# GpSimd's order within a step of the dense products, and 21 instead of 20 window additions per mixing tile

## The chip, the cores and the metric

The kernel runs on one core of one Trainium2 chip. The metric is device time in microseconds (us), the median of several executions. Engines are called PE (TensorE), PEld (its weight load), DVE (VectorE), ACT (ScalarE), POOL (GpSimd) and SP (SyncE, which here only starts transfers).

## The reference

A graph network layer by layer, on 1250 nodes with 1024 features and 40000 edges:

```python
h = jnp.maximum(_layernorm(x, axis=-1), 0.0)
x = x + h @ W.T + bias            # W: 1024 x 1024, W[src, dst] += edge_weight
h = jnp.maximum(_layernorm(x, axis=-1), 0.0)
# two layers on h, with deg the number of edges into a node:
agg = jax.ops.segment_sum(h[src], dst, num_segments=N)
h1 = relu(h @ W_self0 + (agg / max(deg, 1)) @ W_neigh0 + b0)
out = h1 @ W_self1 + (agg(h1) / max(deg, 1)) @ W_neigh1 + b1
x = x + out
```

All in float32. The kernel keeps the precision by splitting each operand into a rounded "hi" part and the rest, "lo", and summing three products of the parts.

## The kernel before

**Stages.** (1) 40 groups of 1000 edges are turned by matmuls into windows: small blocks of the edge-count matrix AT and of the sparse W. The windows of AT go to DRAM (`asum_scratch`) and come back later through a ring of four buffers, `az`. (2) W is turned, and the mixing runs over ten node tiles: x + h @ W.T. (3) Two layers, each with 35 steps of a seven-product scheme for h @ W, and then twenty products with the edge-count matrix (`neighbours`, L1425).

**The seven-product scheme.** Each layer has 7 panels of 5 steps; step v is panel p = (v mod 35) // 5 and row block i = v mod 5. A step is `product(v)`, 24 matmuls of 128x512 on PE (L1383). Its left operand is a transposed block of h, in `stage[v % 2]`, loaded by SP. In the panels p = 2, 3, 5, 6 that operand is first made by POOL from two blocks (`add_operands`, L862, L866, L868 and L871). Then ACT rounds it to hi (`operand_hi`, L1068) and POOL takes operand less hi to get lo (`operand_lo`, L880), into `split[v % 2]`. So the operand of step v + 1 is prepared while PE runs step v; ACT may begin on it only when product(v - 1) has ended, since `split` has two buffers.

**The right operands.** Each panel needs eight blocks of weights, 128x512. They are made one panel ahead, two in each of the steps i = 0 to 3 and none at i = 4 (`blocks_at`). For the panels 2 to 5, so in the steps of the panels 1 to 4, POOL makes a block by a subtraction (`add_blocks`, L895 and L897) from T and `wst`; ACT rounds it (`block_hi`, L1059), DVE takes the rest (`block_lo`, L1734). SP loads the blocks through the ring `wst` of four, each load when the lo of the block four before it is done, and in its queue the operand of step v + 2 stands behind the blocks of step v + 1.

**The window additions.** POOL adds the 288 windows to AT one by one (`add_asums`, L842). Every 16 additions it reads 16 places from the table `tab_a`. The additions are dealt out to 17 slots by `FIRST_ADD`: 40 in slot 0, `MIX_ADDS` each in the slots 1 to 10, the rest of the first 264 over three slots, and 8 each in the last three. In POOL's program the slots 0 to 10 stand in a row ahead of `operand_lo(0)`; slot 11 + v stands in step v. A slot's units (buffers of 4 to 12 windows) are loaded by SP: those of slot i + 1 ahead of right block i + 3 in its queue.

**Who waits.** The engines are separate queues in program order, tied by semaphores. PE's product(v) waits for hi and lo of its operand, at i = 0 also for the eight blocks of its panel, and for the emptied PSUM banks.

Of the kernel before, what the change touches and what calls it, by code (L numbers as in the profile page):

```python
# [19 lines left out]
TN = -(-N // NT)  # L20
# [38 lines left out]
SETS = [(0, 8), (8, 11), (11, 13), (13, 15), (15, 17)] + [(j, j + 1) for j in range(17, LATE)]  # L59
SET_OF = {j: w for w, (a, b) in enumerate(SETS) for j in range(a, b)}  # L60
TURN_ADDS = 40
MIX_ADDS = 20
LATE_AT = 2
FIRST_DEG = 7
AT_TOP = 20
# [10 lines left out]
VL = STEPS * PAIRS  # L76
# [26 lines left out]
NTH = {start: w for w, start in enumerate(STARTS)}  # L103
IN_MIXING = TURN_ADDS + MIX_ADDS * TN
FIRST_ADD = [0] + [TURN_ADDS + MIX_ADDS * i for i in range(TN)]
FIRST_ADD += [IN_MIXING + (len(EARLY_STARTS) - IN_MIXING) * v // (LATE_AT + 1) for v in range(LATE_AT + 2)]
# [3 lines left out]
def build_program(nc, x, x_cols, dst, src_cols, dst_cols, weight_cols, L0_gnn_bias, L1_gnn_W_self0, L1_gnn_W_neigh0,  # L110
# [10 lines left out]
    with ctx:  # L121
# [258 lines left out]
        def used(i, ring):  # L380

            return 16 * (i // ring + 1)


        def parts(v):

            layer, r = divmod(v, VL)
            return layer, r // PAIRS, r % PAIRS

        def op_loaded(v):  # L390

            return 16 * sum(len(LEFT[parts(u)[1]]) for u in range(v % 2, v + 1, 2))

        def nth_sum(v):

            layer, p, i = parts(v)
            return len(LEFT_SUMS) * PAIRS * layer + PAIRS * LEFT_SUMS.index(p) + i

        def source(v):

            layer, p, i = parts(v)
            return S[:, i, :] if p in (2, 3) else stage[:, v % 2, 0, :]
# [18 lines left out]
        def blocks_at(v):  # L421

            layer, p, i = parts(v)
            if p == STEPS - 1:
                return range(0)
            first = WB * (STEPS * layer + p + 1)
            return range(first + BLOCKS_AT[i][0], first + BLOCKS_AT[i][1])
# [40 lines left out]
        def g_at(layer, r):  # L468

            n = r - (VL - TN)  # L470
            return range(2 * TN * layer + n, 2 * TN * layer + n + 1) if 0 <= n < TN else range(0)

        def g_between(layer, o):
            first = 2 * TN * layer + TN
            return range(first + o - 1, first + (TN if o == TN - 1 else o)) if 1 <= o < TN else range(0)
# [11 lines left out]
        def load(eng, row, lo, hi):  # L487

            _, vals = nc.values_load_multi_w_load_instructions(
                row, engines=bass.OrderedEngineSet([eng.engine]), min_val=lo, max_val=hi,  # L490
                skip_runtime_bounds_check_because=clamped)
            return vals
# [16 lines left out]
        def ka(j):  # L509
            return WDS[j] * TN  # L510
# [76 lines left out]
        def adds_in(slot):  # L587
            return STARTS[FIRST_ADD[slot]:FIRST_ADD[slot + 1]] if slot + 1 < len(FIRST_ADD) else []
# [9 lines left out]
        def mix_done(eng):  # L598

            for i in range(TN - 2, TN):  # L600
                eng.wait_ge(s_x1d[i % 2], used(i, 2))
                eng.wait_ge(s_hd[i % 2], used(i, 2))
# [172 lines left out]
        def _(pool):  # L775
# [53 lines left out]
            def add_asums(slot):  # L829

                for j, c in adds_in(slot):
                    n, pos = UNIT_OF[(j, c)]
                    w, entry = NTH[(j, c)], GC * j + c
                    if entry % LOADS == 0:
                        a_bases[:] = load(pool, tab_a[0:1, entry:entry + LOADS], 0, N * TN // 2)
                    if pos == 0 and n < NS_A:
                        pool.wait_ge(s_az[n % NZ], used(n, NZ))
                    elif pos == 0:
                        pool.wait_ge(s_late, n - NS_A + 1)
                    pairs = ka(j) // 2  # L840
                    a = AT32[:, bass.ds(a_bases[entry % LOADS], pairs)]
                    pool.tensor_tensor(a, a, az32[:, n % NZ, pairs * pos:pairs * (pos + 1)], ALU.add) \  # L842
                        ._wait_ge(s_at, w).then_inc(s_at, 1)
# [7 lines left out]
            def add_operands(v):  # L851

                layer, p, i = parts(v)
                if p not in LEFT_SUMS:
                    return
                pool.wait_ge(s_hl[v % 2], op_loaded(v))
                if p == 2:
                    if layer == 0 and i == 0:
                        mix_done(pool)
                    elif i == 0:  # L860
                        pool.wait_ge(s_ag, OL)
                    last = pool.tensor_tensor(S[:, i, :], stage[:, v % 2, 0, :], stage[:, v % 2, 1, :], ALU.add)  # L862
                elif p == 3:
                    pool.wait_ge(s_ohi, v - PAIRS + 1)
                    pool.wait_ge(s_olo, v - PAIRS + 1)
                    last = pool.tensor_tensor(S[:, i, :], S[:, i, :], stage[:, v % 2, 0, :], ALU.subtract)  # L866
                elif p == 5:
                    last = pool.tensor_tensor(stage[:, v % 2, 0, :], stage[:, v % 2, 0, :], stage[:, v % 2, 1, :],  # L868
                                              ALU.subtract)
                else:  # L870
                    last = pool.tensor_tensor(stage[:, v % 2, 0, :], stage[:, v % 2, 0, :], S[:, i, :], ALU.subtract)  # L871
                last.then_inc(s_comb, 1)

            def operand_lo(v):
                if parts(v)[1] in LEFT_SUMS:
                    pool.wait_ge(s_comb, nth_sum(v) + 1)
                else:
                    pool.wait_ge(s_hl[v % 2], op_loaded(v))
                pool.wait_ge(s_ohi, v + 1)
                pool.tensor_tensor(split[:, v % 2, 1, :], source(v), split[:, v % 2, 0, :].bitcast(F32),  # L880
                                   ALU.subtract).then_inc(s_olo, 1)
# [26 lines left out]
            operand_lo(0)  # L908
            for layer in range(2):
                for v in range(VL * layer, VL * (layer + 1)):  # L910
                    ahead = v + 1 < VL * (layer + 1) and v != VL
                    if ahead:
                        add_operands(v + 1)
                    for c in blocks_at(v):
                        add_blocks(c)
                    if ahead:
                        operand_lo(v + 1)
                    add_asums(1 + TN + v)
                    for k in g_at(layer, v % VL - 1):
                        g_lo(k)  # L920
                for k in g_at(layer, VL - 1):
                    g_lo(k)
                for o in range(OL):
                    if layer == 1 and o >= 1:
                        store_out(pool, OL + o - 1)
                    for k in g_between(layer, o):
                        g_lo(k)
                    if layer == 0 and o == OL - 1:
                        operand_lo(VL)
                        operand_lo(VL + 1)  # L930
# [999 lines left out]
```

## Time and profile before

| | |
|---|---|
| median of 3 runs | 816.04 us (814.84 to 818.44) |
| time of the profiled execution | 816.04 us |
| its span | 813.9 us |
| PE busy | 786.5 us, 97% |
| DVE, ACT, POOL busy | 493.6, 366.9, 407.1 us |
| granted TensorE clock, mean | 0.996 of full |

The span is from the first to the last instruction on the core; 2.1 us of the time lie around it. PE is busy in nearly all of the span from 15 us on, so what matters are the few gaps in PE's row and the margin with which the other engines deliver the next step's operand.

### The profile page before, as it was taken

What the parts mean: (1) busy time and instruction counts of PE and PEld (TensorE: products, weight loads), DVE (VectorE), ACT (ScalarE), POOL (GpSimd) and SP (SyncE); (2) the same over time, 40 slices, a digit from 0 to 9 for tenths busy, and PEclk for the clock granted to TensorE, in tenths of its full rate; (3) what the DMA queues carried; (4) which work ended last, traced back from release to release, by engine and by line L of the source; (5) the groups of instructions that cost most, each with busy time, mean ns of one, the idle gap of its engine ahead of it and who ended that gap; (6) DMA issues with size and microseconds to landing.
All of it is one profiled execution on the core that took longest, in us unless ns stands there. A gap on an engine that the chain in (4) does not pass through costs nothing.

```text
span 813.9 us, 13261 instructions
## 1 busy us (share of the span) xinstructions
PE 786.5 (97%) x4533; PEld 638.4 (78%) x4534; DVE 493.6 (61%) x797; ACT 366.9 (45%) x482; POOL 407.1 (50%) x558
## 2 busy tenths in 40 slices
PE   2999999999999999999999999999999999999998
PEld 2766788888778788888877878888888888878886
DVE  7999577778443788876423443235559766246443
ACT  7665643334244232223237876543223223267653
POOL 3000055466758898764752210117899756724310
PEclk9999999999999999999999999999999999999999
DMA  3122455775555853577855643556844669668654
GB/s 109 41 69 80 134 171 168 235 249 165 171 203 187 299 181 90 181 233 244 290 191 175 213 156 106 188 172 213 291 143 142 203 186 340 229 199 267 222 163 140
DMA packets 83127, 151.40 MB, mean 186 GB/s; under 512 B 10965, under 2 KB 21068, under 8 KB 83056
## 3 DMA queue, kind: packets, MB, share of 16 engines
q1 hardware_dynamic: 61354, 102.49, 39.8%
q10 hardware_dynamic: 20182, 43.07, 15.0%
q0 software_dynamic: 1520, 4.92, 1.5%
q8 instruction: 40, 0.66, 0.3%
q14 instruction: 31, 0.25, 0.1%
HBM read 103.79 MB, written 46.65 MB: 185 GB/s over the span
## 4 chain that ended last, share of the span: by engine, by line
PE 86%; DVE 5%; issue 3%; DMA 2%; POOL 2%; ACT 1%; POOLq 0%; ACTq 0%; SPq 0%; DVEq 0%
PE bank L1383 44%; PE bank L1425 20%; PE bank L1318 12%; PE bank L1229 3%; PE bank L1218 3%; PE bank L1234 1%; PE bank L1213 1%; POOL AT L842 1%; PE bank L1441 1%; DVE L L1608 1%; PE bank L1311 1%; DVE R L1594 1%; PE bank L1266 1%; DMA b<-in_L_gnn_b 0%; POOL T L897 0%
## 5 line engine op out<-in xcount | busy, mean ns | idle before, releaser
L1383 PE MATMUL bank<-slot,split 128*128 128x512 f32 x1680 | 387.7, 392 | 3.8 <-issue 2.4
L1383 PEld LDWEIGHTS bank<-slot,split 128*128 128x128 f32 x1680 | 314.9, 189 | 70.1 <-issue 5.2
L842 POOL TENSOR_TENSOR AT<-AT,az 128x50 int32 (+3 forms) x288 | 95.5, 332 | 136.6 <-DMA az<-asum_scratch 97.7
L880 POOL TENSOR_TENSOR split<-stage,split 128x512 fp32r<-128x512 f32 x50 | 65.9, 1319 | 113.0 <-ACT split L1068 112.8
L1100 ACT CAST Ax<-AT 128x1280 fp32r<-128x1280 uint16 x40 | 106.9, 2673 | 32.1 <-PE bank L1425 20.4
L1734 DVE TENSOR_TENSOR slot<-T,slot 128x512 fp32r<-128x512 f32 x64 | 87.5, 1396 | 23.1 <-ACT slot L1059 21.9
L1318 PE MATMUL bank<-slot,split_m 128*128 128x512 f32 x320 | 91.2, 396 | 0.0
L1068 ACT CAST split<-stage 128x512 fp32r<-128x512 f32 x50 | 31.1, 624 | 123.6 <-PE bank L1383 61.1
L1734 DVE TENSOR_TENSOR slot<-wst,slot 128x512 fp32r<-128x512 f32 x48 | 46.6, 997 | 52.9 <-ACT slot L1059 52.9
L1425 PE MATMUL bank<-slot,Ax 128*128 128x512 f32 x320 | 77.2, 393 | 0.2
L1854 DVE SCALAR_TENSOR_TENSOR cst<-bank,dinv,stage 128x512 f32<-128x512 f32 x40 | 30.1, 752 | 72.8 <-PE bank L1425 72.3
L897 POOL TENSOR_TENSOR T<-T,wst 128x512 f32<-128x512 f32 x48 | 70.8, 1491 | 4.1 <-DMA wst<-in_L_gnn_W_self 4.1
L1425 PEld LDWEIGHTS bank<-slot,Ax 128*128 128x128 f32 x320 | 59.3, 188 | 12.9 <-issue 0.8
L1318 PEld LDWEIGHTS bank<-slot,split_m 128*128 128x128 f32 x320 | 58.5, 188 | 11.1
L1213 PE MATMUL bank<-L,R 125*128 125x40 bf16 (+3 forms) x296 | 41.4, 196 | 8.5 <-DVE L L1608 7.0
L1318 PE MATMUL bank<-WTlo,split_m 128*128 128x512 f32 x160 | 49.5, 391 | 0.0
L1425 PE MATMUL bank<-g_first,Ax 128*128 128x512 f32 x200 | 48.6, 389 | 0.0
L1059 ACT CAST slot<-T 128x512 fp32r<-128x512 f32 x64 | 38.1, 619 | 18.1 <-POOL T L897 12.2
L905 POOL TENSOR_TENSOR slot<-cst,slot 128x512 fp32r<-128x512 f32 x16 | 21.6, 1351 | 47.9 <-ACT slot L1115 47.9
L1068 ACT CAST split<-S 128x512 fp32r<-128x512 f32 x20 | 12.4, 622 | 71.8 <-PE bank L1383 63.0
L1213 PEld LDWEIGHTS bank<-L,R 125*128 125x128 bf16 x296 | 29.3, 99 | 19.2 <-issue 13.1
L1425 PEld LDWEIGHTS bank<-g_first,Ax 128*128 128x128 f32 x200 | 37.5, 188 | 7.9
(190 smaller groups left out, 1075.0 us busy)
## 6 DMA issues: line engine op xcount, KB each, us to landing
stage<-hT_scratch SPq DMA_DIRECT2D x90, 256.0 KB, 3.6
wst<-in_L_gnn_W_neigh SPq DMA_DIRECT2D x56, 256.0 KB, 4.7
wst<-in_L_gnn_W_self SPq DMA_DIRECT2D x56, 256.0 KB, 3.1
x1b_scratch<-x ACTq DMA_DIRECT2D x10, 512.0 KB, 5.4
hT_scratch<-hTs ACTq DMA_DIRECT2D x10, 512.0 KB, 3.0
stage<-prod0s_scratch SPq DMA_DIRECT2D x20, 256.0 KB, 2.8
hT_scratch<-h1s ACTq DMA_DIRECT2D x20, 256.0 KB, 3.2
stage<-prod1s_scratch SPq DMA_DIRECT2D x20, 256.0 KB, 2.8
```

The costliest lines, as they stand in the source:

```text
L842: pool.tensor_tensor(a, a, az32[:, n % NZ, pairs * pos:pairs * (pos + 1)], ALU.add) \
L880: pool.tensor_tensor(split[:, v % 2, 1, :], source(v), split[:, v % 2, 0, :].bitcast(F32), ALU.subtract).then_inc(s_olo, 1)
L897: last = pool.tensor_tensor(T[:, b, :], T[:, b, :], wst[:, c % NS, :], ALU.subtract)
L1059: act.copy(slot[t % 2][:, 0, HF * b:HF * (b + 1)], block_source(c)).then_inc(s_whi, 1)
L1068: act.copy(split[:, v % 2, 0, :], source(v)).then_inc(s_ohi, 1)
L1100: act.copy(Ax[:, o % 2, :, :], ATd[:, NT * n:NT * (n + 1), :].rearrange("p d s -> p s d")).then_inc(s_ax, 1)
L1213: last = pe.matmul(a_bank(n)[:, at:at + ka(j)], row, L[:, q, c, 0:ka(j)], start=(c % SHARED[j] == 0), stop=ends)
L1318: last = pe.matmul(bank[2 * (i % 2) + half][0:NT, :], split_m[:, i % 2, a, NT * k:NT * (k + 1)], WT[b][:, k, HF * half:HF * (half + 1)], s ...
L1383: last = pe.matmul(dense_bank(v, which)[:, :], split[:, v % 2, a, NT * k:NT * (k + 1)], slot[t % 2][:, b, HF * (HK * which + k):HF * (HK * ...
L1425: last = pe.matmul(ag_bank(rest_o)[:, :], Ax[:, o % 2, s, :], g_parts(half, s)[:, b, :], start=(s == 0 and b == 0), stop=(s == TN - 1 and ...
L1734: dve.tensor_tensor(lo, block_source(c), hi.bitcast(F32), ALU.subtract).then_inc(s_wlo, 1)
L1854: dve.scalar_tensor_tensor(out=res_tile(o), in0=ag_bank(rest_o)[:, :], scalar=dinv[:, n:n + 1], in1=sums, op0=ALU.mult, op1=ALU.add).then_ ...
```

## The change

`MIX_ADDS` goes from 20 to 21, and in each step of the dense products POOL runs operand_lo(v + 1) directly after add_operands(v + 1), then the window additions, then the right blocks of the step; before, the blocks stood between add_operands and operand_lo, and the additions last.

```diff
-MIX_ADDS = 20
+MIX_ADDS = 21
...
             for layer in range(2):
                 for v in range(VL * layer, VL * (layer + 1)):
-                    ahead = v + 1 < VL * (layer + 1) and v != VL
-                    if ahead:
+                    if v + 1 < VL * (layer + 1) and v != VL:
                         add_operands(v + 1)
-                    for c in blocks_at(v):
-                        add_blocks(c)
-                    if ahead:
-                        operand_lo(v + 1)
-                    add_asums(1 + TN + v)
+                        operand_lo(v + 1)
+                    add_asums(1 + TN + v)
+                    for c in blocks_at(v):
+                        add_blocks(c)
```

The slot bounds become 0, 40, 61, 82, ..., 250, 254, 259, 264 (before 0, 40, 60, 80, ..., 240, 248, 256, 264): 250 instead of 240 additions stand ahead of operand_lo(0), and the slots 11 to 13 have 4, 5 and 5 instead of 8 each.

The order on the engines, at the places that the next part speaks of. First POOL at step 5 of the first layer, before: `T` are two right blocks, `split` is operand_lo, `AT<-AT,az` the last of the window additions.

```order
L842 TENSOR_TENSOR AT<-AT,az 128x50
L897 TENSOR_TENSOR T<-T,wst 128x512 x2
L880 TENSOR_TENSOR split<-stage,split 128x512
L842 ISA
L842 TENSOR_TENSOR AT<-AT,az 128x50
```

The same place in the changed kernel:

```order
L842 TENSOR_TENSOR AT<-AT,az 128x50
L880 TENSOR_TENSOR split<-stage,split 128x512
L842 ISA
L842 TENSOR_TENSOR AT<-AT,az 128x50
L842 ISA
```

The two blocks now come behind the eight additions of that slot. Second, POOL in panel 2 of the first layer, before: `S<-stage` is add_operands.

```order
L862 TENSOR_TENSOR S<-stage 128x512
L895 TENSOR_TENSOR T<-wst,T 128x512 x2
L880 TENSOR_TENSOR split<-S,split 128x512
L862 TENSOR_TENSOR S<-stage 128x512
L895 TENSOR_TENSOR T<-wst,T 128x512 x2
L880 TENSOR_TENSOR split<-S,split 128x512
```

And in the changed kernel:

```order
L862 TENSOR_TENSOR S<-stage 128x512
L880 TENSOR_TENSOR split<-S,split 128x512
L895 TENSOR_TENSOR T<-wst,T 128x512 x2
L862 TENSOR_TENSOR S<-stage 128x512
L880 TENSOR_TENSOR split<-S,split 128x512
L895 TENSOR_TENSOR T<-wst,T 128x512 x2
```

Nothing stands any more between the sum and the subtraction that needs ACT's rounding of that sum.

## Rows read from the trace of the kernel before

**Rows 1.** The page: busy time by engine, and two groups of costly instructions.
```profile
PE 786.5 (97%) x4533; PEld 638.4 (78%) x4534; DVE 493.6 (61%) x797; ACT 366.9 (45%) x482; POOL 407.1 (50%) x558
...
L1734 DVE TENSOR_TENSOR slot<-T,slot 128x512 fp32r<-128x512 f32 x64 | 87.5, 1396 | 23.1 <-ACT slot L1059 21.9
...
L1734 DVE TENSOR_TENSOR slot<-wst,slot 128x512 fp32r<-128x512 f32 x48 | 46.6, 997 | 52.9 <-ACT slot L1059 52.9
```

**Rows 2.** PE in order of time: start, us, instructions, [idle before <- releaser].
```profile
224.45 12.76 PE L1383 MATMUL bank<-slot,split 128*128 128x512 f32 x48 [2.35 <-issue]
...
268.15 5.73 PE L1383 MATMUL bank<-slot,split 128*128 128x512 f32 x24 [1.43 <-POOL split L880]
...
285.23 5.71 PE L1383 MATMUL bank<-slot,split 128*128 128x512 f32 x24
290.91 5.71 PE L1383 MATMUL bank<-slot,split 128*128 128x512 f32 x24
...
532.76 185.39 PE L1383 MATMUL bank<-slot,split 128*128 128x512 f32 x816
```

**Rows 3.** POOL in order of time, in the mixing.
```profile
173.83 2.20 POOL L842 TENSOR_TENSOR AT<-AT,az 128x40 int32 x4 [2.15 <-DMA az<-asum_scratch]
177.19 6.55 POOL L842 TENSOR_TENSOR AT<-AT,az 128x40 int32 x16 [1.17 <-issue]
...
217.29 5.63 POOL L842 TENSOR_TENSOR AT<-AT,az 128x50 int32 x16 [0.93 <-POOL AT L842]
222.89 2.49 POOL L880 TENSOR_TENSOR split<-stage,split 128x512 fp32r<-128x512 f32 x2
```

**Rows 4.** POOL in order of time, steps 5 and 6 of the first layer.
```profile
256.35 2.54 POOL L897 TENSOR_TENSOR T<-T,wst 128x512 f32<-128x512 f32 x2
...
260.55 3.27 POOL L842 TENSOR_TENSOR AT<-AT,az 128x50 int32 x8
...
266.29 1.72 POOL L880 TENSOR_TENSOR split<-stage,split 128x512 fp32r<-128x512 f32 x1
```

**Rows 5.** ACT in order of time, step 5 of the first layer.
```profile
257.13 0.66 ACT L1068 CAST split<-stage 128x512 fp32r<-128x512 f32 x1
```

**Rows 6.** POOL in order of time, panels 2 and 3 of the second layer.
```profile
583.47 1.74 POOL L880 TENSOR_TENSOR split<-S,split 128x512 fp32r<-128x512 f32 x1
585.18 1.74 POOL L862 TENSOR_TENSOR S<-stage 128x512 f32<-128x512 f32 x1
586.88 2.54 POOL L895 TENSOR_TENSOR T<-wst,T 128x512 f32<-128x512 f32 x2
589.38 1.75 POOL L880 TENSOR_TENSOR split<-S,split 128x512 fp32r<-128x512 f32 x1
...
601.18 1.73 POOL L880 TENSOR_TENSOR split<-S,split 128x512 fp32r<-128x512 f32 x1
602.88 1.74 POOL L866 TENSOR_TENSOR S<-S,stage 128x512 f32<-128x512 f32 x1
605.41 1.29 POOL L880 TENSOR_TENSOR split<-S,split 128x512 fp32r<-128x512 f32 x1 [0.80 <-ACT split L1068]
...
610.39 1.31 POOL L880 TENSOR_TENSOR split<-S,split 128x512 fp32r<-128x512 f32 x1
...
628.16 1.77 POOL L880 TENSOR_TENSOR split<-S,split 128x512 fp32r<-128x512 f32 x1
```

**Rows 7.** ACT in order of time, the same stretch.
```profile
582.19 0.62 ACT L1068 CAST split<-S 128x512 fp32r<-128x512 f32 x1 [4.82 <-PE bank L1383]
```

**Rows 8.** SP's transfers in order of time, the same stretch.
```profile
586.34 0.80 SPq L670 DMA_DIRECT2D stage<-hT_scratch  x2
```

**Rows 9.** POOL in order of time, panel 2 of the first layer.
```profile
287.46 1.29 POOL L862 TENSOR_TENSOR S<-stage 128x512 f32<-128x512 f32 x1
288.71 3.46 POOL L895 TENSOR_TENSOR T<-wst,T 128x512 f32<-128x512 f32 x2
...
295.33 1.29 POOL L862 TENSOR_TENSOR S<-stage 128x512 f32<-128x512 f32 x1 [1.91 <-DMA stage<-hT_scratch]
```

## The prediction

> **What bounds the kernel now.** I read the busy times first: PE is busy in 97% of the span [rows 1]. So the kernel can only get faster by closing PE's gaps, and it gets slower wherever an operand comes later than PE wants it. Next, PE's row in order of time over the dense products: two gaps matter here, 2.35 us ahead of product 0, and 1.43 us ahead of product 7, put down to operand_lo [rows 2]. The first is POOL's too, though it is called "issue": POOL's operand_lo(0) and (1) begin at 222.89 and take 2.49 together [rows 3], so the first ends at about 224.1, 0.3 us before PE starts. Together the gaps are 3.8 us, 0.46% of the time. Elsewhere in the products PE runs on without a gap of note, a step each 5.69 us in the first layer (285.23 to 290.91) and 185.39 / 34 = 5.45 us in the second [rows 2]. What decides is whether POOL keeps that pace in the new order.
>
> **Part 1: 21 additions per tile.** Ten more additions stand ahead of operand_lo(0). At the end of the mixing POOL is full: 16 additions begin at 217.29 after 0.93 of reading places, and operand_lo(0) follows at once [rows 3]. Sixteen take 5.63 to 6.55 us there; at the slower pace ten more cost 4.1. The reading of places after addition 240, so far behind operand_lo, now lies bare, 0.9. That is 5.0 us. Against it stands a head start: SP now loads 146 windows ahead of the fourth right block of the mixing, before 140. POOL had 140 done when it waited 2.15 us until 173.83 for the next window, and at 144 it paid 1.17 for places [rows 3]. With six more windows at hand it does those (6 x 6.55 / 16 = 2.5 us) and the reading (1.2) by then: ahead by 3.6, and from there on as full as before. Net: operand_lo(0) begins 5.0 - 3.6 = 1.4 us later, and PE's gap of 2.35 grows by **1.4**. Bounds: 0 if earlier waits for windows give back all of it, 5.0 if none does. The slots 11 to 13 lose these ten additions; POOL waits for ACT in those steps anyway, so that gains nothing.
>
> **Part 2: step 5 and product 7.** Before, POOL did two blocks at 256.35 (2.54), operand_lo(6), eight additions (3.27), two blocks, and operand_lo(7) from 266.29 for 1.72 [rows 4]. Now operand_lo(6) comes first; but ACT's rounding for it ends only at 257.13 + 0.66 = 257.8 [rows 5], and POOL stands until then. From there: lo 1.3, to 259.1; additions 3.3, to 262.4; blocks 2.54, to 265.0. ACT's queue has the rounding of both blocks (0.6 after the second) ahead of operand_hi(7) (0.6), so that ends at 266.3, and operand_lo(7) at 267.7 instead of 268.0. PE gains **0.3**, not 1.43: the blocks of step 5 still stand ahead of operand 7, on ACT. Bounds 0 and 1.43.
>
> **Part 3: the panels 2 and 3, where POOL has sums and blocks.** Before, a cycle of POOL was sum, two blocks, lo. In the second layer, from one operand_lo to the next, it took 589.38 - 583.47 = 5.91 us, and three cycles to 601.18 took 17.7, so 5.90 each, with no idle time [rows 6]: ACT's rounding of the sum ran behind the blocks. In the new order nothing covers it: POOL ends the sum and must wait for ACT before lo. The trace has this very wait where no block lies between: idle 0.80 at 605.41 [rows 6]. So the cycle becomes 5.90 + 0.80 = 6.70 us, against PE's 5.45.
>
> What helps is that operand_lo no longer stands behind the blocks of its own step. From ACT's rounding at 582.19 (+0.62) [rows 7], lo of i = 1 ends at 584.1, where it ended at 585.2 before. PE wants the next ones at 532.76 + 5.45 n [rows 2], less 0.14 from the end of an operand_lo to PE's start (266.29 + 1.72 = 268.01 to 268.15 [rows 2, 4]): 587.1, 592.6, 598.0, 603.5 and, for panel 3, 608.9. They come at 584.1, 590.8, 597.5, 604.2 and 610.9: in time three times, then 0.7 late, then (PE being 0.7 later already) 1.3 late. After i = 4, which has no blocks, sum, wait and lo are 1.74 + 0.80 + 1.30 = 3.84 us: lo at 614.7, wanted at 614.4 + 2.0. Panel 3 had cycles of (628.16 - 610.39) / 3 = 5.92 [rows 6], so 6.7 again: 621.4 is in time by 0.3, 628.1 is 0.9 late, 634.8 is 1.2 late. Sum 0.7 + 1.3 + 0.9 + 1.2 = 4.1.
>
> To that comes SP. A sum's operand is loaded behind right blocks that wait for the lo of the blocks two steps earlier, and in the new order those end some 3 us later (at 586.7 instead of 583.47 for the first pair). The load at 586.34 takes 0.80 to issue [rows 8]; with 3.6 to land (estimate: the page's median for these loads) and 3.2 later it lands at 594.0, where POOL would start the sum at 593.4. One such 0.6 in each panel, somewhat more where PE is already late: 0.9. Second layer: **5.0**. Bounds: with DVE never in POOL's way a cycle is 1.29 + 0.80 + 1.29 + 2.54 = 5.92, which the margins swallow but for 0.5; upper bound in rival (c).
>
> First layer: sum, lo and a block pair of 2.54 or 3.46 make cycles of 5.1 to 6.05 [rows 9], on average 5.6, so 6.4 with the wait, against 5.69. The start leaves 3.4 us of margin (lo of step 11 at 287.3, wanted at 290.8), and four cycles eat 2.9 of it: nothing. At 6.85 a cycle they eat 4.6, 1.2 too much, in each of the two panels. And POOL waited for its operand there already, 1.91 us once [rows 9], which a later load lengthens. Between 0 and 2.4 plus the loads I take **1.5**. Bounds 0 and 5.
>
> The panels 1 and 4 have blocks but no sums, and POOL's 1.3 + 2.5 to 3.5 us fit into a step in either order; the panels 5 and 6 have no blocks on POOL. The blocks' own deadline: a pair of i = 3 ends one lo later, with the whole step i = 4 behind it. All nothing.
>
> **Sum.** 1.4 - 0.3 + 1.5 + 5.0 = 7.6 us on the profiled execution's 816.04 (span 813.9), which is also the median: **823.6 us**, 0.9% slower.
>
> **A page beside the rows.** DVE's L1734 takes 1396 ns where its source is T, which POOL makes, and 997 where it is `wst`; POOL's sum takes 1.29 or 1.74 and its block pair 2.54 or 3.46 [rows 1, 6, 9]. The Trainium skill, "SBUF — State Buffer", section "Who interferes with whom", says that a VectorE instruction with two SBUF inputs and a GpSimd instruction that reads SBUF contend, and that whoever comes second waits for the other's whole instruction. By that, POOL's new idle 0.80 us is time in which DVE's subtraction passes for free: that is rival (a), and it speaks against my sum.
>
> **The rivals.** (a) *The margins hold.* One of the two delays of 0.45 (1.74 - 1.29) in a cycle falls into the new idle time, and the cycle is 6.25. Then the second layer's los come at 584.1, 590.4, 596.6, 602.9 and 609.1, 0.2 late, and 0.9 late once in panel 3; the first layer costs nothing. 816.0 + 1.4 - 0.3 + 1.1 = 818.2. For it: half the first layer's cycles are short already [rows 9]. Against it: in the second none is [rows 6]. Chance 0.23. (b) *Faster.* POOL catches up in the mixing, so that operand_lo(0) comes at ACT's pace and PE's first gap closes, and with operand_lo ahead of the blocks the second closes too: 816.0 - 3.8 = 812.2. The one mechanism is POOL's readiness for operand_lo(0); it decides from the point where the head start is over 5.0 us instead of 3.6, and wins all with 7.4. Against it: from 177.19 on POOL has no more waits for windows to give back. Chance 0.07, of which 0.03 below 812. (c) *Delays in every cycle.* Both long pieces, 1.74 + 0.80 + 1.30 + 3.46 = 7.3 us: 1.85 over the pace. The second layer pays 0.7 + 1.85 + 1.85 and 0.2 + 1.85 + 1.85 = 8.3, the first its 5: 816.0 + 1.1 + 13.3 = 830.4. Chance 0.15. (d) The forecast, 820 to 828: 0.55.
>
> **How the numbers follow.** The likeliest is (d), 823.6. The range takes in most of (a) and reaches up to (c): 816.5 to 830. About 0.5% (4.1 us) is what a measurement of this kernel can tell from no change. Faster: 0.03. Within 0.5%: (a) and the rest of (b), 0.27. Slower than 820.1: (c) and (d), 0.70.
>
> **What would show it.** In the changed profile product 0 starts at about 225.9; the gap ahead of product 7 is near 1.1; in the panels 2 and 3 POOL's operand_lo has an idle time of 0.8 before it, waiting for ACT's L1068; and PE has gaps of 0.7 to 1.3 ahead of the last step of panel 2, the first of panel 3 and the last two of panel 3, in the second layer above all, put down to operand_lo L880. I am wrong if operand_lo(0) starts before 222.9, if the cycles in the second layer's panel 2 stay under 6 us without gaps of PE, or if PE waits for right blocks instead.

## The result, and the profile after

| | before | changed kernel |
|---|---|---|
| median, first measurement | 815.44 us (814.70 to 818.44, 4 runs) | 824.94 us (824.04 to 825.79, 4 runs) |
| ratio, 95% interval | | 1.0109 [1.008, 1.014] |
| median, second measurement | 815.54 us (812.89 to 816.87, 11 runs) | 821.39 us (820.94 to 825.80, 6 runs) |
| ratio, 95% interval | | 1.0072 [1.0059, 1.0085] |
| profiled executions, span | 813.9 us | 816.3 us, 823.7 us |

The change makes the kernel 0.7 to 1.1% slower; 0.9% was forecast. The first profiled execution of the changed kernel is shorter than any of its timed ones: 818.41 us, at full clock. So a second profile, of an execution of 825.80 us, is read beside it (experiment `after_again`).

The page of the changed kernel: busy times, and the groups that answer to [rows 1] (lines after L908 have moved up by two).

```profile
PE 785.7 (96%) x4533; PEld 636.7 (78%) x4534; DVE 474.8 (58%) x797; ACT 370.4 (45%) x482; POOL 391.2 (48%) x558
...
L1732 DVE TENSOR_TENSOR slot<-T,slot 128x512 fp32r<-128x512 f32 x64 | 71.4, 1115 | 91.8 <-ACT slot L1057 87.3
```

The same work takes DVE 18.8 us and POOL 15.9 us less than before; PE gains nothing by it. What PE waited for, from the waits of the changed kernel (us in all, how often, the longest):

```profile
PE bank L1404 <- DVE degs L1782: 3.1, 4, 1.3
PE bank L1381 <- issue: 2.8, 1, 2.8
...
PE bank L1381 <- POOL split L880: 1.3, 2, 0.8
PE bank L1381 <- DVE q L1811: 0.6, 1, 0.6
```

In the kernel before, `product` waited only 2.35 and 1.43 us [rows 2]. PE of the changed kernel in order of time:

```profile
224.50 11.13 PE L1381 MATMUL bank<-slot,split 128*128 128x512 f32 x48 [2.82 <-issue]
...
265.69 5.70 PE L1381 MATMUL bank<-slot,split 128*128 128x512 f32 x24 [0.54 <-POOL split L880]
272.16 0.35 PE L1404 MATMUL bank<-one,degs 128*128 128x1 f32 x2 [0.77 <-DVE degs L1782]
...
278.82 0.38 PE L1404 MATMUL bank<-one,degs 128*128 128x1 f32 x2 [0.66 <-DVE degs L1782]
...
286.11 0.38 PE L1404 MATMUL bank<-one,degs 128*128 128x1 f32 x2 [1.33 <-DVE degs L1782]
...
604.84 5.70 PE L1381 MATMUL bank<-slot,split 128*128 128x512 f32 x24 [0.79 <-POOL split L880]
611.18 109.52 PE L1381 MATMUL bank<-slot,split 128*128 128x512 f32 x480 [0.64 <-DVE q L1811]
```

Three groups of gaps. Ahead of product 0 it is 2.82 us instead of 2.35; ahead of product 7, 0.54 instead of 1.43. Then come three that did not exist, ahead of the products 8, 9 and 10 (0.77, 0.66, 1.33), put down to the degree sums of DVE. A fourth of this kind, 0.32 us, is ahead of product 15. And there are two at the end of panel 2 of the second layer. The products 0 and 1 took 11.13 us here and 12.76 before: the clock was full here.

POOL of the changed kernel in panel 2 of the second layer, answering to [rows 6]:

```profile
583.67 1.29 POOL L880 TENSOR_TENSOR split<-S,split 128x512 fp32r<-128x512 f32 x1 [0.80 <-ACT split L1066]
584.92 2.55 POOL L895 TENSOR_TENSOR T<-wst,T 128x512 f32<-128x512 f32 x2
587.41 1.75 POOL L862 TENSOR_TENSOR S<-stage 128x512 f32<-128x512 f32 x1
589.96 1.29 POOL L880 TENSOR_TENSOR split<-S,split 128x512 fp32r<-128x512 f32 x1 [0.80 <-ACT split L1066]
...
594.20 1.29 POOL L862 TENSOR_TENSOR S<-stage 128x512 f32<-128x512 f32 x1 [0.46 <-DMA stage<-hT_scratch]
...
600.89 1.74 POOL L862 TENSOR_TENSOR S<-stage 128x512 f32<-128x512 f32 x1 [0.80 <-DMA stage<-hT_scratch]
603.42 1.28 POOL L880 TENSOR_TENSOR split<-S,split 128x512 fp32r<-128x512 f32 x1 [0.80 <-ACT split L1066]
```

Every operand_lo of the panel now has the forecast 0.80 us of idle time before it. But the cycle is 6.29 us (583.67 to 589.96), not 6.70, since operand_lo is short (1.29) each time. Two transfers came late (0.46 and 0.80), as forecast.

### The profile page after: what moved, and what is told of

Its sections match the earlier page's. It is cut to its first block, busy times and chain, and to the rows that moved or that the text cites. A ratio compares the mean times of both kernels' runs of the same rounds, so it can differ in the third digit from the quotient of the medians.

```text
span 816.3 us, 13261 instructions
## 1 busy us (share of the span) xinstructions
PE 785.7 (96%) x4533; PEld 636.7 (78%) x4534; DVE 474.8 (58%) x797; ACT 370.4 (45%) x482; POOL 391.2 (48%) x558
## 3 DMA queue, kind: packets, MB, share of 16 engines
q0 software_dynamic: 1520, 4.92, 1.5%
## 4 chain that ended last, share of the span: by engine, by line
PE 76%; POOL 6%; DVE 6%; issue 5%; DMA 3%; ACT 3%; SPq 1%; ACTq 0%; POOLq 0%; DVEq 0%
PE bank L1381 33%; PE bank L1423 21%; PE bank L1316 12%; PE bank L1216 3%; PE bank L1227 3%; DMA stage<-hT_scratch 2%; POOL T L897 2%; POOL T L895 2%; POOL S L862 2%; PE bank L1232 1%; PE bank L1211 1%; DVE L L1606 1%; ACT split L1066 1%; PE bank L1439 1%; PE bank L1309 1%
## 5 line engine op out<-in xcount | busy, mean ns | idle before, releaser
L842 POOL TENSOR_TENSOR AT<-AT,az 128x50 int32 (+3 forms) x288 | 92.4, 321 | 135.8 <-DMA az<-asum_scratch 93.7
L1732 DVE TENSOR_TENSOR slot<-T,slot 128x512 fp32r<-128x512 f32 x64 | 71.4, 1115 | 91.8 <-ACT slot L1057 87.3
L1098 ACT CAST Ax<-AT 128x1280 fp32r<-128x1280 uint16 x40 | 107.1, 2677 | 31.6 <-PE bank L1423 20.8
L1057 ACT CAST slot<-T 128x512 fp32r<-128x512 f32 x64 | 39.8, 622 | 110.1 <-POOL T L897 83.4
L1732 DVE TENSOR_TENSOR slot<-wst,slot 128x512 fp32r<-128x512 f32 x48 | 44.9, 961 | 51.4 <-ACT slot L1057 51.2
L1423 PEld LDWEIGHTS bank<-slot,Ax 128*128 128x128 f32 x320 | 59.2, 188 | 12.7 <-issue 0.7
L1316 PEld LDWEIGHTS bank<-slot,split_m 128*128 128x128 f32 x320 | 58.5, 188 | 11.1
L1066 ACT CAST split<-stage 128x512 fp32r<-128x512 f32 x50 | 31.1, 624 | 76.0 <-POOL stage L871 28.7
L897 POOL TENSOR_TENSOR T<-T,wst 128x512 f32<-128x512 f32 x48 | 61.0, 1293 | 0.0
L1211 PEld LDWEIGHTS bank<-L,R 125*128 125x128 bf16 x296 | 29.1, 98 | 19.2 <-issue 13.1
L1216 PE MATMUL bank<-L,R 125*128 125x32 bf16 (+3 forms) x888 | 43.3, 191 | 0.1
```

Source lines behind the costliest of these rows:

```text
L897: last = pool.tensor_tensor(T[:, b, :], T[:, b, :], wst[:, c % NS, :], ALU.subtract)
L1057: act.copy(slot[t % 2][:, 0, HF * b:HF * (b + 1)], block_source(c)).then_inc(s_whi, 1)
L1066: act.copy(split[:, v % 2, 0, :], source(v)).then_inc(s_ohi, 1)
L1098: act.copy(Ax[:, o % 2, :, :], ATd[:, NT * n:NT * (n + 1), :].rearrange("p d s -> p s d")).then_inc(s_ax, 1)
L1211: last = pe.matmul(a_bank(n)[:, at:at + ka(j)], row, L[:, q, c, 0:ka(j)], start=(c % SHARED[j] == 0), stop=ends)
L1216: last = pe.matmul(w_bank(j)[:, bass.ds(offsets[c // SHARED[j]], kw(j))], row, L[:, q, c, ka(j) + kw(j) * part:ka(j) + kw(j) * (part + 1)] ...
```

## The experiments

All were timed beside the kernel before, in four series. Beside the ratio I give two figures, means over the executions of a kernel: the time **lost to the clock**, span x (1 - granted clock), and the **rest**, span x granted clock. For the kernel before they are 2.0 to 2.4 us and 810.9 to 812.0 us, by series; each difference is taken within a series.

The division is rough, for two reasons. The granted clock can be low while PE waits anyway: in `mix21_only` it is 0.74 in the gap ahead of product 0 itself (222.22 to 227.12 us), and this counts 1.3 us as lost to the clock that is plain waiting. And in eleven of the fourteen profiles another 1.7 us of the first figure lies at 30 to 50 us, far from the change (0.83 in ten of these microseconds).

### The two halves apart

`mix21_only`, the kernel before with one edit:

```diff
-MIX_ADDS = 20
+MIX_ADDS = 21
```

> The kernel before with MIX_ADDS = 21 alone; POOL's order in the dense steps is as before. My sum: POOL is full at the end of the mixing, so operand_lo(0) comes 1.4 us later and the time is 0.2% over before (1.000 to 1.004). Rival, from the profile of the changed kernel, where operand_lo(0) began at 222.94 as before at 222.89: the head start pays the ten additions whole, the ratio is 1.000 and operand_lo(0) begins at 222.9.

`order_only`, the changed kernel with

```diff
-MIX_ADDS = 21
+MIX_ADDS = 20
```

> The changed kernel with MIX_ADDS back at 20: the new order alone. If the order costs all, the ratio to before is 1.007 to 1.011 and PE shows gaps of 0.3 to 1.3 us in the steps 7 to 11 of the first layer and at the end of panel 2 in the second. If the number of additions has a part in it, by what it moves in the steps 0 to 6, the ratio is under 1.005.

Measured: `mix21_only` 1.0037 [1.0024, 1.0050], rest +1.3 us, clock +1.6 us. `order_only` 1.0069 [1.0047, 1.0092], rest +5.4, clock +0.8. Together 1.0106, which the first measurement of the changed kernel (1.0109) bears out; the second (1.0072) is at the lower edge of the two intervals. In the rest the second agrees, +6.1 us against 1.3 + 5.4. So both halves lose, and the order seems to lose more.

PE in `mix21_only`, and then PE's granted clock there. In the second fence, as in all of its kind below, a row is a stretch: its length, PE's busy time (matmuls), **granted clock**, DMA share, GB/s.

```profile
227.12 13.15 PE L1383 MATMUL bank<-slot,split 128*128 128x512 f32 x48 [4.90 <-issue]
```

```profile
205.00:222.00 17.00, 17.00 (x85) 1.00 0.41 134
222.00:240.00 18.00, 13.10 (x51) 0.81 0.63 201
240.00:258.00 18.00, 18.00 (x97) 1.00 0.67 219
```

The gap ahead of product 0 has grown from 2.35 to 4.90 us, and the clock, full before it, is 0.81 after it: some of the next matmuls ran at the lower of the two levels (1.2 instead of 2.4 GHz), so that 48 of them took 13.15 us instead of the 11.13 at full clock. Where the gap comes from, in POOL:

```profile
174.09 5.61 POOL L842 TENSOR_TENSOR AT<-AT,az 128x40 int32 x14 [3.87 <-DMA az<-asum_scratch]
...
207.06 5.70 POOL L842 TENSOR_TENSOR AT<-AT,az 128x50 int32 x16 [0.90 <-POOL AT L842]
215.60 5.63 POOL L842 TENSOR_TENSOR AT<-AT,az 128x50 int32 x16 [2.84 <-issue]
222.16 3.53 POOL L842 TENSOR_TENSOR AT<-AT,az 128x50 int32 x10 [0.93 <-POOL AT L842]
```

The ten more additions cost 3.53 + 0.93 = 4.5 us, against 5.0 forecast. The head start came: addition 160, the last of the row at 174.09, was done at 179.70, before at 183.74 [rows 3, the 16 additions from 177.19], so 4.0 us ahead. But it did not last. Addition 240, the last of the row at 215.60, was done at 221.23, before at 222.92 [rows 3, from 217.29]: 1.7 us ahead. The readings of places on the way took up to 2.84 us, where they mostly take 0.9. So operand_lo(0) started 4.5 - 1.7 = 2.8 us later, at 225.65. The stall of 2.84 us ahead of 215.60 is also in the second profile of the changed kernel (2.71), not in the first:

```profile
211.59 6.94 POOL L842 TENSOR_TENSOR AT<-AT,az 128x50 int32 x16 [0.92 <-POOL AT L842]
```

There addition 240 was done at 218.53, 4.4 us ahead, and operand_lo(0) started at 222.94, hardly later than before (222.89 [rows 3]). What makes the stall is open; the trace names no releaser.

### The order, by panels

`early_only` has the new order only in the panels 0 and 1 of both layers, `panels23_only` only in 2 and 3; both with 20 additions.

```diff
+                    lo_first = parts(v)[1] < 2      # panels23_only: in (2, 3)
                     if ahead:
                         add_operands(v + 1)
+                        if lo_first:
+                            operand_lo(v + 1)
+                    if lo_first:
+                        add_asums(1 + TN + v)
                     for c in blocks_at(v):
                         add_blocks(c)
-                    if ahead:
+                    if ahead and not lo_first:
                         operand_lo(v + 1)
-                    add_asums(1 + TN + v)
+                    if not lo_first:
+                        add_asums(1 + TN + v)
```

> MIX_ADDS = 20, the new order in the panels 0 and 1 only (of both layers), the old one from panel 2 on. If the sums' panels 2 and 3 carry the loss, as I forecast (1.5 + 5.0 us), this is 0.996 to 1.001. If the loss sits in panel 1 of the first layer, where the changed kernel shows PE waiting for DVE's degree sums for 3.1 us in all, this is 1.003 to 1.006.

> MIX_ADDS = 20, the new order in the panels 2 and 3 only, the old one elsewhere. My forecast: 6.5 us in these, ratio 1.008, with PE's gaps at the end of panel 2 in the second layer. Rival: the cycle of 6.3 us in the changed profile is mostly covered by the margins, 1.5 to 3 us in all, ratio 1.002 to 1.004.

Measured: `early_only` 1.0045 [1.0028, 1.0062], rest +3.1; `panels23_only` 1.0027 [1.0013, 1.0042], rest +2.3. The rests add up to the 5.4 of `order_only`, so the new order in panel 4, which is in neither, costs nothing that shows. More than half of the order's cost comes from the panels 0 and 1, for which the prediction had a gain of 0.3; the panels 2 and 3 cost 2.3 instead of 6.5.

### Is it the window additions, or the degree sums?

`lo_first_adds_last` keeps operand_lo ahead of the blocks but puts the additions behind the blocks, with 20 per tile:

```diff
                     if ahead:
                         add_operands(v + 1)
+                        operand_lo(v + 1)
                     for c in blocks_at(v):
                         add_blocks(c)
-                    if ahead:
-                        operand_lo(v + 1)
                     add_asums(1 + TN + v)
```

> MIX_ADDS = 20; in each step operand_lo directly after add_operands, then the right blocks, then the window additions. It differs from the run with the whole new order (1.0069) only in the steps 0 to 5, where there are additions. If the eight additions ahead of the blocks of step 5 start the delays of panel 1, most of the loss of panel 1 (about 3.7 us) goes: ratio 1.002 to 1.004. If the blocks being behind operand_lo is enough, it stays at 1.006 to 1.008.

Measured: 1.0056 [1.0034, 1.0077], rest +4.3, below the 1.006 that was given for "it stays", and above the 1.004 of the other case. The gap ahead of product 7 is gone, but the waits for the degree sums stay, 2.0 us in four. What the additions ahead of the blocks cost, 5.4 - 4.3 = 1.1 us, is within the noise: the intervals of the two runs overlap. They are not the main cause.

`deg20` moves the degree sums, which PE seems to wait for, from the steps 7 on to the steps 20 on, behind the panels that are in question; `early_deg20` does that and the order of `early_only`.

```diff
-FIRST_DEG = 7
-AT_TOP = 20
+FIRST_DEG = 20
+AT_TOP = 32
```

> The kernel before with the degree sums (DVE's count_edges and PE's small matmuls) moved from the steps 7 to 17 to the steps 20 to 30. It is the base for the next one. The same work in other steps; the products of the panels 1 to 3 come faster by 0.25 us each, so POOL may fall behind a little there: 0.998 to 1.003.

> The same later degree sums with the new order in the panels 0 and 1 only. The new order there cost 1.0045 with the degree sums in place. If PE loses that time by waiting for DVE's degree sums, which stand behind block_lo in DVE's queue, this is within 0.001 of the run with later degree sums alone. If it is the operand that comes late (its load on SP stands behind the loads of the right blocks, which wait for block_lo), it stays 0.003 to 0.005 above that run, and PE's gaps in the steps 8 to 10 are put down to operand_lo or ACT.

Measured: `deg20` 0.9996 [0.9981, 1.0011]; `early_deg20` 1.0068 [1.0043, 1.0093], rest +5.5, more than without the move. PE in `early_deg20`, from product 7:

```profile
265.43 5.70 PE L1389 MATMUL bank<-slot,split 128*128 128x512 f32 x24 [0.54 <-POOL split L880]
271.82 5.70 PE L1389 MATMUL bank<-slot,split 128*128 128x512 f32 x24 [0.68 <-POOL split L880]
278.13 5.72 PE L1389 MATMUL bank<-slot,split 128*128 128x512 f32 x24 [0.61 <-POOL split L880]
```

The gaps ahead of the products 7, 8 and 9 stand where they stood, now put down to operand_lo; ahead of product 10 there are 0.62 us instead of 1.33, put down to DVE. So the theory that the degree sums are the cause falls for the products 8 and 9: they only came last in a step in which the operand came late as well. Ahead of product 10 they do bear a part. There operand_lo(10) was done at 283.71 + 1.29 = 285.00 in the changed kernel, 1.1 us before the degree sum's matmuls began at 286.11:

```profile
283.71 1.29 POOL L880 TENSOR_TENSOR split<-S,split 128x512 fp32r<-128x512 f32 x1 [0.80 <-ACT split L1066]
```

The move itself costs something with the new order: the profile of `early_deg20` has a gap of 0.94 us ahead of product 13 that `early_only` does not have. A likely reason is that PE asks sooner for each operand without them: seven products in a row took 38.38 us in `deg20`, 5.48 each, against 5.69 [rows 2].

### The loop through SP's queue

ACT of the changed kernel, the rounding of the operands 8 and 9:

```profile
270.26 0.62 ACT L1066 CAST split<-stage 128x512 fp32r<-128x512 f32 x1 [1.56 <-DMA stage<-hT_scratch]
...
276.67 0.63 ACT L1066 CAST split<-stage 128x512 fp32r<-128x512 f32 x1 [1.22 <-DMA stage<-hT_scratch]
```

It waits for the operand's own transfer. In the kernel before, no rounding waited for a transfer in these steps. SP of the changed kernel:

```profile
264.94 0.43 SPq L652 DMA_DIRECT2D wst<-in_L_gnn_W_self  x1
265.49 0.35 SPq L670 DMA_DIRECT2D stage<-hT_scratch  x1
...
270.37 0.47 SPq L652 DMA_DIRECT2D wst<-in_L_gnn_W_self  x1
270.95 2.21 SPq L670 DMA_DIRECT2D stage<-hT_scratch  x3
```

And the same load of operand 8 in the kernel before:

```profile
261.58 0.43 SPq L652 DMA_DIRECT2D wst<-in_L_gnn_W_self  x1
262.13 0.35 SPq L670 DMA_DIRECT2D stage<-hT_scratch  x1
```

The buffer of operand 8 is free as soon as operand_lo(6) is done, at 256.36 + 1.28 = 257.6 in the changed kernel. Its load is issued at 265.49, 7.9 us later, directly behind right blocks. Those wait for the lo of the blocks of step 5, which now come from POOL at 260.39 instead of 256.35 [rows 4]. So the load is 3.4 us later, the data are there at about 270.2, and ACT's rounding starts with them; POOL waits 2.98 us for it ahead of operand_lo(8):

```profile
271.02 1.27 POOL L880 TENSOR_TENSOR split<-stage,split 128x512 fp32r<-128x512 f32 x1 [2.98 <-ACT split L1066]
```

The same goes for every step with blocks: the blocks of step u are ahead of the load of operand u + 3. Before, POOL made these blocks ahead of operand_lo(u + 1), so the way round was from operand_lo(u) over the blocks of step u, block_lo, SP's queue and ACT to operand_lo(u + 3): three steps of PE, 17 us. Now they stand behind operand_lo(u + 1), and it is two steps: 11.4 us. One turn of it in the changed kernel, from operand_lo(7) at 264.25 over the blocks of step 6 and the load of operand 9 at 270.95 to operand_lo(9) at 277.44, took 13.2 us, longer than PE's two steps, so PE has to wait. POOL's rows of it:

```profile
264.25 1.29 POOL L880 TENSOR_TENSOR split<-stage,split 128x512 fp32r<-128x512 f32 x1 [1.32 <-ACT split L1066]
265.50 2.54 POOL L897 TENSOR_TENSOR T<-T,wst 128x512 f32<-128x512 f32 x2
...
277.44 1.28 POOL L880 TENSOR_TENSOR split<-stage,split 128x512 fp32r<-128x512 f32 x1 [2.64 <-ACT split L1066]
```

The test is to take the operand's load out of the loop. `order_sp_first` is `order_only` with SP's two loads of a step swapped, `sp_first` the kernel before with the same swap:

```diff
+                    if v + 2 < VL * (layer + 1):
+                        load_operand(v + 2)
                     if v + 1 < VL * (layer + 1):
                         for c in blocks_at(v + 1):
                             load_block(c)
-                    if v + 2 < VL * (layer + 1):
-                        load_operand(v + 2)
```

> The new order in all steps, MIX_ADDS = 20, and SP loads the operand of step v + 2 ahead of the right blocks of step v + 1 instead of behind them. The new order alone cost 1.0069. Theory: a loop over two steps sets the pace of panel 1: operand_lo(7), blocks, ACT's and DVE's part, SP's queue, the load of operand 9, its rounding, operand_lo(9), 12.7 us instead of 11.4. With the operand's load no longer behind the blocks' the loop is cut: panel 1 loses nothing, PE has no gaps in the steps 8 to 10, ratio 1.001 to 1.004 (the panels 2 and 3 stay, 2 us or less). Rival: POOL's and DVE's queues alone make the delay; it stays at 1.006 to 1.008.

> The kernel before with SP's two loads swapped as in the run beside it. Base for it: no gaps of PE in the old order hang on an operand's load, so 0.998 to 1.002. If the right blocks, now loaded later, are next, it is slower, and the run beside it must be read against this one.

Measured: `order_sp_first` 1.0030 [1.0011, 1.0048], rest +1.6; `sp_first` 1.0007 [0.9993, 1.0021], rest +0.4. The order costs 1.6 - 0.4 = 1.2 us where SP loads the operand first, and 5.4 where it doesn't; the 5.4 is from another series. One part of the expectation failed: PE still has a gap ahead of product 8. ACT, SP, POOL and PE of `order_sp_first`:

```profile
271.46 0.62 ACT L1066 CAST split<-stage 128x512 fp32r<-128x512 f32 x1 [0.34 <-issue]
```

```profile
260.13 0.33 SPq L670 DMA_DIRECT2D stage<-hT_scratch  x1
...
268.35 0.33 SPq L670 DMA_DIRECT2D stage<-hT_scratch  x1
```

```profile
272.23 1.30 POOL L880 TENSOR_TENSOR split<-stage,split 128x512 fp32r<-128x512 f32 x1 [1.75 <-ACT split L1066]
```

```profile
274.59 0.35 PE L1404 MATMUL bank<-one,degs 128*128 128x1 f32 x2 [0.75 <-DVE degs L1782]
```

Operand 8 is loaded at 260.13, right behind operand_lo(6), and its rounding waits for no transfer any more. POOL still waits 1.75 us ahead of operand_lo(8): that is ACT's queue, where the blocks' rounding stands ahead of the operand's. So the 0.75 us ahead of product 8, the same as without the swap (0.78 in `order_only`), don't hang on the load. What the swap takes away comes behind it: ahead of the products 9 and 15 no gap is left, ahead of product 10 0.20 us of 0.53. Of the second layer's two gaps, 0.70 and 0.64, 0.30 us is left. In PE's rows that makes some 1.9 us less than in `order_only`'s; the rests of the two differ by 3.8.

### The other direction, and a version that is faster

`mix19` is the kernel before with

```diff
-MIX_ADDS = 20
+MIX_ADDS = 19
```

> The kernel before with MIX_ADDS = 19. With 21 the runs gave 1.0037. If POOL's additions ahead of operand_lo(0) set product 0's start, ten fewer open the gap less: 1 to 3 us off, ratio 0.996 to 0.999, PE's gap ahead of product 0 near 1 us, and its clock no longer falls after it. If 21 costs by what it moves out of the steps 0 to 2, or if ACT's rounding is next at once, the ratio is 1.000 to 1.002.

Measured: 0.9981 [0.9966, 0.9997], rest -0.7, clock -1.1. PE in `mix19`, with the stretch of its clock behind:

```profile
246.71 5.69 PE L1383 MATMUL bank<-slot,split 128*128 128x512 f32 x24 [1.01 <-POOL split L880]
...
265.81 5.69 PE L1383 MATMUL bank<-slot,split 128*128 128x512 f32 x24 [1.72 <-POOL split L880]
```

```profile
222.00:240.00 18.00, 18.00 (x92) 1.00 0.71 235
```

The gap ahead of product 0 is gone and the clock stays full, but a good part comes back: POOL has the ten additions later, and PE waits 1.01 us ahead of product 4 and 1.72 ahead of product 7. `best` spreads them: 12, 14 and 8 in the slots 11 to 13, and the eight additions of step 5 behind operand_lo(7).

```diff
-MIX_ADDS = 20
+MIX_ADDS = 19
...
-FIRST_ADD += [IN_MIXING + (len(EARLY_STARTS) - IN_MIXING) * v // (LATE_AT + 1) for v in range(LATE_AT + 2)]
+FIRST_ADD += [IN_MIXING, IN_MIXING + 12, IN_MIXING + 26, len(EARLY_STARTS)]
...
-                    add_asums(1 + TN + v)
+                    if v != 5:
+                        add_asums(1 + TN + v)
+                    if v == 6:
+                        add_asums(1 + TN + 5)
```

> The kernel before with 19 additions per mixing tile, the three slots behind it at 12, 14 and 8 additions, and the 8 additions of step 5 moved behind operand_lo(7), so that operand_lo(7) comes from POOL about 2 us earlier. If the gaps ahead of products 4 and 7 in the kernel with 19 additions (1.0 and 1.7 us) come from these additions alone, both close, and with the gap ahead of product 0 closed too the span less the time lost to the clock is 808 to 810 us against 811.8 before, ratio 0.994 to 0.998. If the rounding of operand 7 on ACT, which stands behind the right blocks' rounding, is what is late there, the gap ahead of product 7 stays over 1 us and the ratio is 0.998 to 1.000.

Measured: 811.20 us against 815.54, ratio 0.9949 [0.9937, 0.9961], rest -3.5, clock -0.8. PE in `best`:

```profile
222.01 11.14 PE L1386 MATMUL bank<-slot,split 128*128 128x512 f32 x48
...
251.51 16.60 PE L1386 MATMUL bank<-slot,split 128*128 128x512 f32 x72
...
268.78 5.73 PE L1386 MATMUL bank<-slot,split 128*128 128x512 f32 x24 [0.56 <-POOL split L880]
```

The gaps ahead of the products 0, 4 and 7 are closed; one of 0.56 us is left, ahead of product 8. The old gaps were 2.35 + 1.43 = 3.8 us; 3.8 - 0.56 = 3.2 of the 3.5 us are explained by them. The rest of the executions is 807.4 us, a little under the 808 to 810 expected.

### The changed kernel again

> The changed kernel once more, to see in a profile what the longer executions do. The two halves of the change were measured apart at +0.37% (21 additions) and +0.69% (order), so their sum asks for a ratio of 1.007 to 1.013. If the part of the 21 additions that the gap alone doesn't explain (1.3 us of gap, 3.0 of time) is TensorE's clock after a longer gap, a profile whose gap ahead of product 0 is over 3 us shows the 48 matmuls behind it at 12.8 to 13.6 us and a granted clock near 0.8 in 222 to 240 us; the rival, that the clock has nothing to do with the gap, expects 11.1 us there as in the first profile of this kernel, or the slow ones behind a short gap. If SP's queue is what costs in panel 1, TensorE waits in 265 to 320 us some 3 to 4 us in all for L1404's degrees and operand_lo L880, as in that first profile.

PE in this longer execution, and its clock:

```profile
226.92 13.06 PE L1381 MATMUL bank<-slot,split 128*128 128x512 f32 x48 [4.92 <-issue]
...
276.51 0.35 PE L1404 MATMUL bank<-one,degs 128*128 128x1 f32 x2 [0.79 <-DVE degs L1782]
...
289.76 0.38 PE L1404 MATMUL bank<-one,degs 128*128 128x1 f32 x2 [1.02 <-DVE degs L1782]
```

```profile
222.00:240.00 18.00, 13.08 (x51) 0.81 0.61 208
```

As in `mix21_only`, the gap is 4.92 us and the clock 0.81. The waits in 265 to 320 us are 0.54 + 0.79 + 0.33 + 1.02 + 0.32 = 3.0 us, in the first profile 0.54 + 0.77 + 0.66 + 1.33 + 0.32 = 3.6; the second layer's two gaps are again 0.79 and 0.64. So the loop and the second layer are alike in both, and they differ at product 0: gap and matmuls together 18.0 us against 14.0. That is 4.0 of the 7.4 us between the two spans. Of the others 2.4 are waits of the neighbours' products for ACT's L1098, 2.9 against 0.5 us in all; they range from 0.5 to 2.9 us over the profiles of all kernels, `order_only` and `early_only` at 1.5 and 0.6 among them, and I count none of them as an effect of the change.

## Why the prediction was right, and where its terms were wrong

The total was right: 823.6 us forecast, 824.94 and 821.39 measured, and slower by over 0.5% in both. Its terms were not, and that the total fits is luck: Part 1 was 1.6 us too low and the panels 0 and 1 were 3.4 too low, while the panels 2 and 3 were 4.2 too high.

**Part 1, forecast 1.4 us, measured 3.0** (1.0037 of 816). The price of the additions and the size of the head start were nearly right: 4.5 and 4.0 us instead of 5.0 and 3.6. What failed is "from there on as full as before": of the 4.0 us only 1.7 were left at addition 240 in `mix21_only`, so operand_lo(0) came 2.8 us later. The profile accounts for the 3.0: the gap ahead of product 0 is 4.90 - 2.35 = 2.55 us longer, and the 48 matmuls behind it take 13.15 - 12.76 = 0.39 longer, a cost of the clock that the sum had at nothing. In the first profile of the changed kernel 4.4 us of head start were left, and product 0 began at 224.50, not at the forecast 225.9; in the other two it began at 226.92 and 227.12. How often the stall comes in the timed executions is not known. The rest of +1.3 us looks like the 1.4 of the sum, but that is no proof of it: part of the longer wait is counted under the clock.

**Part 2, forecast -0.3, measured -0.9.** The gap ahead of product 7 went from 1.43 to 0.54 (0.52 in `order_only`), where 1.1 was forecast; that what remained would be ACT's queue was right: POOL waits 1.32 us there for L1066.

**"The panels 1 and 4 … All nothing" is the step that failed.** It weighed POOL's time in a step (1.3 + 2.5 to 3.5 us) and not what depends on it in a queue. Part 3 had the mechanism for the panels 2 and 3, "a sum's operand is loaded behind right blocks that wait for the lo of the blocks two steps earlier", and priced it 0.9 us; the same sentence holds in panel 1, where it closes the loop. With Part 2's gain, the panels 0 and 1 cost 3.1 us instead of -0.3. The swap on SP takes away 3.8 of the order's 5.4 us (5.4 to 1.6); how these 3.8 divide between panel 1 and the others was not tried. And the loop through SP is not all of panel 1: the gap ahead of product 8 stays with the swap, on ACT's queue, and DVE's queue has a part ahead of product 10.

**Part 3, forecast 6.5, measured 2.3.** Idle 0.80 before each operand_lo: right. Gaps ahead of the last step of panel 2 and the first of panel 3 in the second layer: right in place and time (604.84 and 611.18), 0.79 and 0.64 us instead of 0.7 and 1.3. The second is put down to DVE, but operand_lo ended only 0.2 us before PE began (609.69 + 1.29 = 610.98). Panel 3's two gaps never came, because the cycle there is 6.28 and not 6.7. That is the mechanism of rival (a), which was given 0.23: one of a cycle's two delays of 0.45 falls into the new idle time. L1734, which is L1732 after, shows it from DVE's side: 1396 ns before [rows 1], 1115 after. The rule of the Trainium skill that was cited for it ("SBUF — State Buffer", "Who interferes with whom") agrees with that number in that the two engines contend. That the second waits for the whole instruction of the other is not shown: operand_lo is 0.45 us longer or not at all, and DVE's subtraction alone takes 0.96 to 1.0. No number of the sums above depends on it.

Rival (b) was wrong as to this change, but its price was about right: with both gaps closed the kernel takes 811.2 us (`best`), and 812.2 was given for it. It needed fewer additions ahead of operand_lo(0), not more.

Left open: the stall of 2.7 to 2.8 us in POOL at 213 us; and a part of the 5.4 us of `order_only`'s rest. The gaps of the changed kernel's first profile for the order (2.8 + 0.3 + 1.4 - 0.9) make only 3.6, those of `order_only`'s own profile (2.4 + 1.3 - 1.4) only 2.3. That profile also has a gap of 3.68 us ahead of product 0, 1.3 more than before, though nothing that the order changes runs before it. So the start of product 0 varies by itself, and how much of the 5.4 us is that can't be said from one profile.

## What to carry to other kernels

When work is moved back on one engine, follow what it frees: the loads that wait for those buffers, and everything that stands behind these loads in the same queue. An engine with spare time in each step can still be part of a loop over several steps that is slower than the bottleneck. In such a loop a transfer whose buffer is free should not stand behind one whose buffer isn't; in the old order, where the loop had three steps, the same swap gained nothing (1.0007). The engine named for a wait is the last of several; moving its work away, as `early_deg20` did, tells whether it is the cause. A gap of the bottleneck that can be traced to work of no urgency, as the window additions ahead of operand_lo(0), is closed by dealing that work out against each step's own margin.

## What the runs showed of the hardware

**The clock can fall with a gap of a few us, and the matmuls behind it then take 1.5 to 2.4 us more.** Gap ahead of product 0, and granted clock in 222 to 240 us, in fourteen profiles: no gap (`mix19`, `best`), 1.00. Gaps of 2.3 to 2.8 us, 1.00 in three and 0.91 in six. 3.68 us (`order_only`), 4.90 and 4.92 us, 0.81. The 48 matmuls behind it took 11.1 to 11.2 us at 1.00, 12.7 to 12.8 at 0.91 and 13.1 to 13.6 at 0.81. PE had been busy from 205 us up to the gap, at full clock. The length of the gap alone doesn't decide: 2.82 us went by at full clock, 2.32 us once did and once didn't. The three profiles with a gap and the full clock are also the only ones of all fourteen without the lower clock at 30 to 50 us; why is not shown. In the long gaps the clock was at its lower level 1.7 to 2.8 us before the matmuls began (0.50 in 225 to 231 us in `mix21_only`, whose matmuls began at 227.12).

**POOL waits 0.80 us for a rounding of 0.62 us.** From the end of the sum on POOL to the start of operand_lo it is 0.80 us in each cycle of panel 2 shown above; the hand-over to ACT and back costs some 0.2 us beyond ACT's own 0.62.

**The new order made the same instructions faster.** DVE was busy 474.8 instead of 493.6 us and POOL 391.2 instead of 407.1, for the same instructions; with the order alone (`order_only`) it was 474.2 and 394.3. POOL's 48 subtractions at L897 took 61.0 instead of 70.8 us. That the two engines overlap less is the likely reason, but no run here tried it by itself. Busy times that fall are no sign of a faster kernel: PE had gained nothing.
